# Layer 0 of a gated four-layer model: another order of turned values, residual, v's chunks and normalised rows

## What is computed

```python
q = visual_tokens @ wq.T + bq            # visual_tokens = layernorm(x)
res = q
k = top_k_report_tokens @ wk.T + bk      # the context, 375 rows
v = top_k_report_tokens @ wv.T + bv
attn = softmax(einsum('bhqd,bhkd->bhqk', qh, kh) * d ** (-0.5))   # 8 heads of 32
out = einsum('bhqk,bhkd->bhqd', attn, vh)
out = _layernorm(res + out, ln_g, ln_b)
return _kan_linear(out, kan_base_w, kan_spline_w, kan_spline_scaler, _grid())
# _kan_linear: silu(out) @ base_w.T + splines(out) @ scaled_spline_w.T
# then: x = x + tanh(g_xattn[0]) * result
```

## Time and profile before

| what | us |
|---|---|
| median of 3 runs | 2767.51 |
| lowest and highest | 2767.16, 2771.26 |
| the profiled execution | 2766.18 |
| its span, first to last instruction | 2764.4 |
| first and last update of x in layer 0 | 91.0, 411.5 |

### The profile page before, as it was taken

How to read it: one execution, slowest core, us unless ns; L and a number is a source line. 1 busy time by engine, 2 the same in 40 slices (tenths; PEclk the granted TensorE clock), 3 DMA queues, 4 the chain that set the end, 5 groups by cost and what they waited for, 6 DMA issues and landing times. The chain is left out here.

```text
span 2764.4 us, 56714 instructions
## 1 busy us (share of the span) xinstructions
PE 2617.9 (95%) x19818; PEld 1981.6 (72%) x19818; DVE 1547.1 (56%) x4177; ACT 1296.0 (47%) x3610; POOL 642.0 (23%) x626
## 2 busy tenths in 40 slices
PE   6999978999999999989899998999998999989998
PEld 4777756666666666656677766999995777768887
DVE  4777856555555555535787874333235887742222
ACT  4777743343434334331567663333335777732222
POOL 0666661000000000000444431222221111013232
PEclk9999989999999999999999999999999999999999
DMA  3000002000000000010000006999991000059897
GB/s 119 17 23 18 12 2 109 13 13 8 13 7 13 7 13 7 1 34 1 20 18 19 23 7 244 324 334 327 323 326 46 24 18 24 7 201 312 303 312 224
DMA packets 91811, 267.57 MB, mean 97 GB/s; under 512 B 25068, under 2 KB 50804, under 8 KB 77268
## 3 DMA queue, kind: packets, MB, share of 16 engines
q1 hardware_dynamic: 74356, 242.53, 25.4%
q0 software_dynamic: 13632, 18.62, 3.2%
q10 hardware_dynamic: 3616, 3.67, 0.4%
HBM read 248.13 MB, written 16.65 MB: 96 GB/s over the span
## 5 line engine op out<-in xcount | busy, mean ns | idle before, releaser
L825 PEld LDWEIGHTS a_full_ps<-ident,a_probs 112*125 112x125 f32 x2688 | 369.9, 190 | 122.6 <-issue 59.8
L1926 PEld LDWEIGHTS m_banks<-m_x_inT,m_w 128*128 128x128 f32 x3824 | 435.1, 192 | 15.2 <-issue 13.5
L1926 PE MATMUL m_banks<-m_x_inT,m_w 128*128 128x128 f32 x3824 | 442.2, 276 | 1.4 <-ACT m_x_inT L1997 0.9
L936 ACT ACTIVATE a_probs<-a_masked,a_negmax 112x375 f32<-112x375 f32 x512 | 305.4, 598 | 287.7 <-DVE a_negmax L1151 287.7
L825 PE MATMUL a_full_ps<-ident,a_probs 112*125 112x112 f32 x2688 | 417.5, 281 | 16.7 <-ACT a_pT L943 5.6
L1177 DVE COPY a_pT<-a_full_ps 125x448 f32<-125x448 f32 x448 | 277.4, 621 | 233.9 <-PE a_full_ps L825 231.9
L725 PE MATMUL a_full_ps<-attention_room 128*125 128x256 f32 (+1 forms) x960 | 330.0, 472 | 9.6 <-ACT a_qT L926 3.7
L717 PE MATMUL a_full_ps<-attention_room 128*128 128x375 f32 x896 | 325.0, 491 | 13.8 <-PEq L1769 8.6
L1151 DVE CUSTOM_DVE_ANT_0 a_masked<-a_sc_ps,a_mask_add 112x375 f32<-112x375 f32 x512 | 249.7, 544 | 33.2 <-PE a_sc_ps L812 32.0
L936 ACT ACTIVATE a_probs<-a_sc_ps,a_negmax 112x375 f32<-112x375 f32 x384 | 216.6, 575 | 89.4 <-DVE a_negmax L1157 89.3
L843 PEld LDWEIGHTS a_o_ps<-a_pT,a_v 125*32 125x32 f32 (+1 forms) x5376 | 165.2, 118 | 127.0 <-issue 98.7
(11 more groups left out here) (253 smaller groups left out, 3473.3 us busy)
## 6 DMA issues: line engine op xcount, KB each, us to landing
m_w<-in_L2f_w SPq DMA_DIRECT2D x105, 1024.0 KB, 6.4
m_w<-in_L3f_w SPq DMA_DIRECT2D x72, 768.0 KB, 5.9
attention_room<-in_ctxT SPq DMA_DIRECT2D x64, 375.0 KB, 3.1
m_w<-in_L3f_w SPq DMA_DIRECT2D x36, 640.0 KB
m_b<-in_L2f_b SPq DMA_DIRECT2D x35, 128.0 KB, 8.0
p_rows<-normed SPq DMA_DIRECT2D x16, 224.0 KB, 6.2
attention_room<-in_L0x_spline_wT SPq DMA_DIRECT2D x1, 2048.0 KB, 10.5
net_room<-in_L1f_w SPq DMA_DIRECT2D x2, 1024.0 KB
```

Of the source, the lines that this page charges most:

```text
L825: mm = pe.transpose(full_ps[0:KT, bank_of["turn", i, k], (j % 4) * S:(j % 4 + 1) * S], probs[:, i % 2, a, t * KT:(t + 1) * KT], ident[0:S, ...
L936: act.activation(probs[:, i % 2, a, 0:SK], src, ACT.Exp, bias=negmax[:, m:m + 1], scale=-1.0 if mask else 1.0, accum_out=rowsum[:, par, n: ...
L1926: mm = pe.matmul(ab_ps[:, (par * FC + f) % RING, i * SLOTS:(i + 1) * SLOTS], w[:, par, c, f * P:(f + 1) * P], x_inT[:, c, :], start=(c == ...
```

## The change

It does three things in layer 0. In the table, the turned values (`oback`) move from behind q to behind k's first chunk, and on the last place of the second group the empty entry comes first and the turned q last. In DVE's body, the residual goes ahead of the copy of the second turned piece and the variance ahead of the copy of the third. And the normalised rows, of x for batch t + 2 and of the net for batch t - 3, are written ahead of the update, not behind it.

```diff
 CYCLES = {
-    0: [[[("xT",)], [("k", 0)], [("q", 0), ("oback",)], [("v", 0, 0), ("k", 1)]],
-        [[], [], [("kan",), ("lnt",)], [("v", 1, 0), ("qtok",), ("v", 2, 0), ("rest",)]]],
+    0: [[[("xT",)], [("k", 0), ("oback",)], [("q", 0)], [("v", 0, 0), ("k", 1)]],
+        [[], [], [("kan",), ("lnt",)], [("rest",), ("v", 1, 0), ("v", 2, 0), ("qtok",)]]],
...
                     if exists(t - 2):
                         kan_cube(t - 2, 0)
+                    if exists(t - 1):
+                        kan_residual(t - 1)
                     if exists(t):
                         copy_turn(t, 0, 1)
                     if exists(t - 1):
-                        kan_residual(t - 1)
+                        kan_variance(t - 1, 1 - par)
                     if exists(t):
                         copy_turn(t, 0, 2)
-                    if exists(t - 1):
-                        kan_variance(t - 1, 1 - par)
                     if exists(t - 2):
                         kan_cube(t - 2, 1)
                         kan_silu(t - 2)
...
                         norm_stats(t + 2)
+                        norm_apply(t + 2)
+                    if early(t - 3):
+                        norm_net.apply(dve, t - 3, t - 3)
                     if exists(t - 2):
                         update(t - 2, full_ps[:, bank_of[("kan",)], :])
                     if exists(t):
                         copy_turn(t, 1, 2)
-                    if exists(t + 2):
-                        norm_apply(t + 2)
                     copies(t, par, 1, 3)
                     if exists(t - 2):
                         row_stats(t - 2)
-                    if early(t - 3):
-                        norm_net.apply(dve, t - 3, t - 3)
```

## The result

The changed kernel takes 2780.01 us (median of 6 runs, 2778.27 to 2784.98), the kernel before 2767.92 (6 runs): 1.0043 times as long, 95% interval 1.003 to 1.0056. It is slower by 12.1 us, where 8.2 were forecast. The profiled execution took 2780.8 us with a span of 2779.0, against 2766.18 and 2764.4: 14.6 us more.

| | before | after | difference |
|---|---|---|---|
| until the first update | 91.04 | 94.42 | +3.38 |
| first to last update, layer 0's loop | 320.51 | 328.78 | +8.27 |
| behind it, code that the change doesn't touch | 2352.82 | 2355.77 | +2.95 |
| span | 2764.4 | 2779.0 | +14.6 |

What follows compares the result with a forecast made beforehand. Two equally long loops, PE's and one through DVE and POOL, were taken to bound the kernel. A round of 21.70 + 0.54 + 0.1 = 22.34 us, together 8.2 us, gave 2775.8 us, range 2766 to 2781.

Steps and rivals of the forecast that it cites:

- Steps 1 and 2: PE: v's second chunk no longer follows the update, gain 0.30 us; v's first chunk no longer awaits q's copy, 0.33.
- Step 3: PE: q waits for ACT's copy of k's first chunk, 0.64 us a round; PE's sum 0.0, its loop stays 21.7.
- Step 4: DVE: residual's add held until POOL's add of bases ends; the copy behind it adds 0.54 us a round.
- Step 5: DVE: both normalised rows move into the 3.2 us before the update and can hold POOL; 0.1 us a round.
- Step 6: PE: v's third chunk and turned q swap places; cost nothing, 0.15 us cover. Row statistics of x later, nothing.
- The first: Rival: DVE's add runs free beside POOL, PE binds alone and its terms cancel; 2767.5 us within 2; chance 0.22.
- The second: Rival: rows ahead of the update take the port from POOL's power and square, 0.4 us later; 2779.7 us; chance 0.22.
- The third: Rival: q doesn't wait and the add is free, PE keeps both gains, 8.2 us; 2759.3 us; chance 0.10.

Runs made afterwards that it cites:

- short bases: Changed kernel with POOL's adds of bases cut to one of the eight bases, most of the splines' part left out; 2765.64 us, one run.
- e8_root_later: Table change alone with ACT copying k before its exponentials, POOL's net root moved behind squares and cubes, net's row one batch later; 2783.03 us.
- k first: Changed kernel with ACT copying k's first chunk ahead of the exponentials of the first two heads; 2777.27 us, one run.
- e11_q_third: As e10_both_loops, but with the net's root and row where they stood in the kernel before; 2763.62 us.
- e10_both_loops: Kernel before with q one place later, turned values earlier, ACT copying k first, DVE's variance after residual and copies, net's root and row later; 2762.22 us.

## Why the prediction was right, and where it was off

The sign, the loop and the chain came out: 8.2 us were worked out for the loop, 8.3 measured; 2775.8 us for the whole, 2780.0 measured, inside the range. That 8.2 and 8.3 lie so close is in part luck: the full rounds gave 1.4 us less than forecast and the draining ones 1.5 more, for which no experiment was made. Of the 12.1 us in all, 3.8 lie beyond the loop, in parts that the sum did not have.

**Steps 1 and 2** hold as far as they go. The waits behind the update and behind ACT's copy of q are gone, and are worth nothing in this kernel, since PE isn't what bounds the loop any more.

**Step 3**: the wait is 0.53, not 0.64 us, and PE's own loop is 21.59 (the kernel with short bases), not 21.70. The step missed two things. One is DVE: taken alone, the table does not cancel out, since in DVE's old order the copy of the third piece waits for what q delays (22.11 us a round, not 21.7). In the changed kernel this cost and that of step 4 are not added: with the variance back the round falls by 0.17 only. The other is the first filled round, where the same wait is 3.21 us. I had taken its size from a steady round; at the start ACT's queue is held by maxima that come late.

**Step 4** was right in mechanism and size. Add held to POOL's end plus 0.27 (0.28 forecast), copy behind it for 0.53 (0.54). One detail was off: the add of the first round with splines is held as well (1.49 us, the shortest of the thirteen). Without the rows the round is 0.47 longer than before (22.17 against 21.70), for 0.54. The Trainium skill, Advanced Engine Details and Errata, VectorE Performance Modes, names only GpSimd instructions and 2p Vector instructions as blocking each other; the add, which is none of the latter, took 1.78 against 0.41 us all the same. The GPSIMD Details of the same page in the Trainium skill name instructions with two SBUF inputs too, and the trace agrees.

**Step 5** was right in size (0.11 and 0.07 measured for 0.1) and wrong in its picture. I had the row of x at 0.4 to 0.6 us and it takes 2.28; the update was in time only because the 3.2 us hole before it was just long enough: the row and the net's take 247.46 to 250.06 and the update starts at 249.99. Its bounds also had no term for the start, where there is no such hole and the row adds 2.4 us to a wait of PE (4.88 against 2.45 to 2.47). That wait and the one for k are the two new ones ahead of the first update, which came 3.4 us later; the sum put nothing there.

**Step 6** was wrong: I left v's third chunk 0.15 us of cover, and did not take off the 0.30 us by which step 1 brings PE there sooner. The row of waits shows what is left, 0.24 us a round of weight load behind the last copy. It costs nothing here only because PE has slack.

**The rivals.** The first (add free) would need what the short bases made: there the add is free and the round is 21.59 us. In the changed kernel POOL shuts it out. The second named a time close to the measured one, 2779.7, for a reason that didn't occur: POOL's powers stay at 0.55 us and its cube is 0.15 us longer, not 0.4. The third fell with the wait at L740.

**Still open.** The 3.0 us behind layer 0 go with the clock: the stretches at the 1.2 GHz level behind the last update add up to 62.1 us before and 62.2 in the kernel with the rows back (2352.8 and 2352.7 us of work), 72.4 in the changed kernel (2355.8), 82.4 in e8_root_later (2359.3), and the other profiles lie between. The code there is the same in all. Why a kernel meets more or less of it there isn't settled; in the changed kernel it was the same in both profiles. Nor is it settled how the 3.4 us at the start divide between the two waits and the clock: each of five kernels that differ from the changed one in some part (the table alone, variance back, rows back, short bases, k first) has its first update between 89.0 and 91.8 instead of at 94.3.

## What to carry to other kernels

When a DVE operation of the kinds that were held here (an add of two SBUF tiles, a tile scaled into another) is issued while POOL works, ask when POOL ends, not when DVE is free: moving it ahead wins nothing, and what is put behind it is paid. Put copies from PSUM into that time instead; beside the same POOL operation they ran at full speed. And price a new wait, or a row moved into a hole, at the loop's start too: there the engine that ends the wait may be held by something that the steady round doesn't have (3.21 us instead of 0.53 here), and the hole may be missing.

## What the runs showed of the hardware

- The hold lasts until POOL's instruction ends, and a little more: 0.27 to 0.29 us for the add of two tiles (1.78 against 0.41), 0.14 to 0.16 for the row of x.
- An operation with one SBUF tile as its input is held too, and by two POOL instructions in a row: the row of x waited through the end of L188 and all of L624, 2.28 us against 0.41. By the Trainium skill, VectorE: DVE Perf Modes, What auto-detection actually checks, VectorE takes the mode with both ports (2×_2P) if a single source and the destination are in SBUF and their outermost dimensions are both even, as they are here (256). The trace agrees in that the row is held like an operation that needs the shared port; the mode itself shows in no row.
- The copies from PSUM weren't held: 0.61 us at 257.12 within POOL's add of bases, and 1.14 for two at 265.46 (e11_q_third). The statistics of a row (L1198), which read SBUF, weren't either: 0.41 us at 252.82 within POOL's square (251.97, 1.68 us).
- It goes the other way too: POOL's cube beside DVE's net row took 2.24 us instead of 2.09, and POOL's root L619, issued during DVE's second cube, takes 1.33 us (e10_both_loops, at 267.55), against 0.55 where the copy stands ahead of that cube (changed kernel, at 260.72).
- Who is held can turn on hundredths of a microsecond. In the changed kernel the net's row starts 0.10 or 0.11 us ahead of POOL's cube in eleven rounds and takes 0.40 us; in e8_root_later it starts 0.06 to 0.08 ahead in nine and takes 2.29 to 2.31.
